# Raw cosine and sine tables turned once, the bias added in head 0, the causal mask on VectorE, fewer scatter drains, and powers three tiles behind

## The reference

```python
q  = rope(rmsnorm(x @ Wq + bq, qn_w), pos)            # per head
entries = sum over 4 tokens of softmax(x @ Wcmp + bcmp) * x      # 512 entries
ck = rope(rmsnorm(entries @ Wk + bk, kn_w), block_ends);  cv = entries @ Wv + bv
sc = q @ ck.T * scale, NEG where block_ends > pos;  top 8 of each row, softmax over them, times cv
lk = rope(rmsnorm(x @ Wlk + blk, kn_w), pos);  lv = x @ Wlv + blv
local = softmax(q @ lk.T over the own and the previous block of 128, banded) @ lv
x  = layernorm(x + ((sparse + local) / 2) @ Wo + bo)
```

```python
y = sum over the 4 picked experts of weight * (silu(x @ w1[e]) * (x @ w3[e])) @ w2[e]
x = layernorm(x + y + (silu(x @ sw1) * (x @ sw3)) @ sw2)
```

## Time and profile before

| what | us |
|---|---|
| median of three executions (2488.65 to 2490.56) | 2489.43 |
| the profiled execution, its own time | 2492.0 |
| its span, first to last instruction | 2490.2 |
| TensorE busy, share of the span | 2239.0 (90%) |
| VectorE busy | 1372.6 (55%) |
| ScalarE busy | 1172.2 (47%) |
| GpSimd busy | 1348.1 (54%) |

### The profile page before, as it was taken

The page is one execution under the profiler, slowest core; times in us unless marked ns, Lnnn a source line. Parts: engine busy times, 40 slices in busy tenths (PEclk is TensorE's granted clock), DMA queues, the critical chain, the costliest instruction groups (busy, mean ns, idle before and its releaser), DMA issues. The chain is left out here.

```text
span 2490.2 us, 45317 instructions
## 1 busy us (share of the span) xinstructions
PE 2239.0 (90%) x13489; PEld 2017.7 (81%) x13490; DVE 1372.6 (55%) x4446; ACT 1172.2 (47%) x3726; POOL 1348.1 (54%) x1942
## 2 busy tenths in 40 slices
PE   5299999999999999999999996989799999878662
PEld 3289999899899999898999995867699998768542
DVE  4266676676666667666666776382223323343257
ACT  2166666566566666666666665421133333333211
POOL 2576676666666666666666664436501103483374
PEclk8599999999999999999999999689899999989876
DMA  3140060000000000000000001214523324564164
GB/s 119 62 171 3 28 266 13 11 20 18 5 20 18 5 21 20 16 8 21 19 4 20 2 1 41 75 42 167 188 80 112 112 80 144 174 203 151 66 192 146
DMA packets 68916, 178.29 MB, mean 72 GB/s; under 512 B 11648, under 2 KB 15296, under 8 KB 68672
## 3 DMA queue, kind: packets, MB, share of 16 engines
q1 hardware_dynamic: 36864, 85.58, 10.4%
q0 software_dynamic: 19568, 69.10, 8.5%
q10 hardware_dynamic: 12240, 20.73, 2.3%
HBM read 108.26 MB, written 67.13 MB: 70 GB/s over the span
## 5 line engine op out<-in xcount | busy, mean ns | idle before, releaser
L773 POOL TENSOR_TENSOR cross<-nat,rope_tables 128x128 f32<-128x128 f32 x256 | 147.9, 578 | 446.0 <-DVE nat L635 446.0
L921 PE MATMUL bank<-whi,xT_lo 128*128 128x384 f32 x1024 | 368.7, 360 | 4.2 <-ACT v L727 3.3
L922 PE MATMUL bank<-wlo,xT_hi 128*128 128x384 f32 x1024 | 347.2, 339 | 0.0
L923 PE MATMUL bank<-whi,xT_hi 128*128 128x384 f32 x1024 | 346.4, 338 | 0.0
L1475 POOL TENSOR_TENSOR ring_lo<-staged,ring_hi 128x1088 fp32r<-128x1088 f32 x48 | 121.2, 2538 | 402.4 <-ACT ring_hi L1437 398.3
L597 DVE TENSOR_TENSOR acc<-acc,bank 128x512 f32<-128x512 f32 x256 | 176.0, 688 | 226.7 <-PE bank L923 210.0
L707 ACT COPY probT<-bank 128x128 f32<-128x128 f32 (+3 forms) x256 | 109.1, 426 | 380.2 <-PE bank L549 380.2
L921 PE MATMUL bank<-ring_hi,xslo 128*128 128x352 f32 x600 | 205.1, 342 | 29.1 <-issue 27.7
L635 DVE TENSOR_TENSOR nat<-bank,bqk 128x256 f32<-128x256 f32 x256 | 108.9, 426 | 165.0 <-PE bank L923 163.9
L921 PEld LDWEIGHTS bank<-whi,xT_lo 128*128 128x128 f32 x1024 | 193.0, 188 | 4.8 <-DVE nat L635 3.6
L923 PE MATMUL bank<-ring_hi,xshi 128*128 128x352 f32 x600 | 196.5, 328 | 0.0
(11 more groups left out here) (295 smaller groups left out, 6349.2 us busy)
## 6 DMA issues: line engine op xcount, KB each, us to landing
staged<-in_wexp POOLq DMA_DIRECT2D x60, 544.0 KB, 5.2
slots_in<-zeros SPq DMA_DIRECT2D x41, 512.0 KB, 6.0
xslot<-slots_in SPq DMA_DIRECT2D x76, 256.0 KB, 2.7
slots_out<-yslot ACTq DMA_DIRECT2D x76, 256.0 KB, 2.0
wraw<-in_wh SPq DMA_DIRECT2D x16, 768.0 KB, 4.3
staged<-in_wexp SPq DMA_DIRECT2D x20, 544.0 KB, 3.8
slots_out<-zeros SPq DMA_DIRECT2D x9, 512.0 KB, 6.1
acc<-in_x SPq DMA_DIRECT2D x4, 1024.0 KB, 14.1
```

Source lines behind the costliest of these rows:

```text
L773: pool.tensor_tensor(cross[:, :, :], nat[:, a.two, :, 0:2 * ROT], sin, ALU.mult).then_inc(s_mult, 1)
L921: pe.matmul(out, wl_, xh_, start=first, stop=False)
L922: pe.matmul(out, wh_, xl_, start=False, stop=False)
L923: return pe.matmul(out, wh_, xh_, start=False, stop=last)
```

## The change

Opening: the raw tables are loaded in one piece, cosines in rows 0 to 63 and sines in rows 64 to 127 of `cos_sin`, and turned once, one transpose a tile, between the second and the third block of entries. The norm weights are turned too (two transposes, one ScalarE copy, `nw`), and VectorE multiplies the turned tables out of the bank into `rope`, two products a chunk. GpSimd fills the 64 columns that are not turned with the norm weight and makes `cos_end` and `sin_end` from the raw tables; the second half of the sines for these comes when the first is used, by a wait on SP. ScalarE's high parts of the first head's weights stand ahead of the entry copies, GpSimd's low parts ahead of the power. VectorE's rope of the compressed keys stands ahead of the mean of squares, and the last chunk's low parts behind it. `bo` is added by GpSimd, one tile a step, in head 0, and VectorE's output sums of head 0 wait for it.

Heads: the mask matmul is gone; VectorE adds `diag`, now float32, to the last 32 score columns in the bank, and its memset waits for that. The reversed view of the sines is gone.

Front: GpSimd waits after every sixteenth transfer instead of every eighth. Combine: power(n) stands behind gather(n+3). The diff, cut; what is left out are names in signatures, semaphores and tile declarations.

```diff
@@ -98,27 +98,27 @@
-    diag = sb("diag", [P, EPT], BF16)
-    identb = sb("identb", [P, P], BF16)
+    diag = sb("diag", [P, EPT])
+    bo = sb("bo", [P, HID])
...
@@ -183,13 +180,18 @@
             for c in range(NCH):
                 sp.dma_start(acc[:, c * TPC:(c + 1) * TPC, :],
                              t["x"][c * CH:(c + 1) * CH, :].rearrange("(n p) d -> p n d", p=P)).then_inc(x_in[c], 16)
+            sp.dma_start(cos_sin[0:2 * ROT, :], t["cos"][0:2 * ROT, :]).then_inc(tab_in, 16)
+            sp.dma_start(cos_sin[2 * ROT:4 * ROT, :], t["sin"][2 * ROT:4 * ROT, :]).then_inc(tab_in, 16)
             sp.dma_start(wk[:, :, :], t["Wk"].rearrange("(k p) d -> p k d", p=P)).then_inc(k_in, 16)
+            sp.dma_start(sin[:, :], t["sin"][0:2 * ROT, 0:S // 2]).then_inc(sin_in, 16)
             sp.dma_start(wraw[:, :, :, :].rearrange("p a k d -> p (a k d)"), t["wh"][0, :, 0:3 * KC * D]).then_inc(w_in, 16)
-            sp.dma_start(bo[:, :], t["bo"].broadcast_to([P, HID])).then_inc(r_in, 16)
+            sp.dma_start(bo[:, :], t["bo"].broadcast_to([P, HID])).then_inc(bo_in, 16)
                              t["wh"][h, 0:1, 3 * KC * D + 2:HEAD_COLS].rearrange("o d -> d o")).then_inc(blv_in[h], 16)
+            sp.wait_ge(ends_done, 2)
+            sp.dma_start(sin[:, :], t["sin"][0:2 * ROT, S // 2:S]).then_inc(sin_in, 16)
             sp.wait_ge(bias_copy, 1)
...
             x_highs(0)
             act.wait_ge(bias_turn, 1)
             act.copy(bias_by_head[:, :], bank[0][0:2 * NH, 0:P]).then_inc(bias_copy, 1)
+            act.wait_ge(nw_turn, 1)
+            act.copy(nw[:, :, :], bank[1][:, 0:2 * P].rearrange("p (g d) -> p g d", g=2)).then_inc(nw_copy, 1)
+            act.copy(cos_end[2 * ROT:P, :], norm_w[2 * ROT:P, 0:1].to_broadcast([P - 2 * ROT, C])).then_inc(nw_copy, 1)
             act.wait_ge(wstep, 4)
             act.activation(by_tile[:, :], by_tile[:, :], ACT.Exp).then_inc(wexp, 1)
             for b in range(CB):
                 act.wait_ge(ent, b + 1)
                 act.copy(rows[:, b, :], bank[b][:, :]).then_inc(ent_rows, 1)
             x_highs(1)
+            act.wait_ge(w_in, 16)
+            for k in range(KC):
+                act.copy(weight_piece(whi[0], k), wraw[:, :, k, :]).then_inc(w_high, 1)
             for k in range(0, KC, 2):
                 act.wait_ge(ent_turned, k + 1)
                 act.copy(entT[:, k, :], bank[k][:, :]).then_inc(ent_act, 1)
...
         @block.tensor
-                    wait_for(pe, x_low, (c - 1) * KC + k + 1)
+                    if c == 1:
+                        pe.wait_ge(tab_sin, k + 1)
+                    else:
+                        wait_for(pe, x_low, (c - 1) * KC + k + 1)
...
-            def tables(c):
-                pe.wait_ge(tab, c + 1)
-                for i in range(TPC):
-                    if c:
-                        pe.wait_ge(tab_copy, (c - 1) * TPC + i + 1)
-                    else:
-                        pe.wait_ge(x_low, (NCH - 1) * KC + i + 1)
-                    cols = slice(i * P, (i + 1) * P)
-                    for j, src in enumerate((cosq, cosk, sin)):
-                        mm = pe.transpose(bank[4 + i][:, j * P:(j + 1) * P], src[:, cols], ident[:, :])
+            def tables():
+                pe.wait_ge(tab_in, 32)
+                for c in range(NCH):
+                    pe.wait_ge(x_low, c + 1)
+                    for i in range(TPC):
+                        n = c * TPC + i
+                        mm = pe.transpose(bank[4 + c][:, i * P:(i + 1) * P], cos_sin[:, n * P:(n + 1) * P], ident[:, :])
                     mm.then_inc(tab_turn, 1)
...
                          ident[:, :]).then_inc(bias_turn, 1)
+            pe.wait_ge(c_in, 16 * 6)
+            pe.transpose(bank[1][:, 0:P], norm_w[:, 1:2].to_broadcast([P, P]), ident[:, :])
+            pe.transpose(bank[1][:, P:2 * P], norm_w[:, 0:1].to_broadcast([P, P]), ident[:, :]).then_inc(nw_turn, 1)
...
             pe.wait_ge(bias_copy, 1)
+            pe.wait_ge(nw_copy, 1)
             for b in range(CB):
+                if b == 2:
+                    tables()
                 pe.wait_ge(wspread, b + 1)
...
         @block.gpsimd
-            def tables(c):
-                cols = slice(c * CH, (c + 1) * CH)
-                if c:
-                    pool.wait_ge(tab_turn, c * TPC)
-                pool.dma_start(cosq[:, :], t["cos"][:, cols]).then_inc(cos_in, 16)
-                pool.dma_start(sin[:, :], t["sin"][:, cols]).then_inc(sin_in, 16)
-                pool.wait_ge(cos_in, (c + 1) * 16)
-                pool.wait_ge(sin_in, (c + 1) * 16)
-                if not c:
-                    pool.wait_ge(c_in, 16 * 6)
-                pool.tensor_scalar(cosk[:, :], cosq[:, :], norm_w[:, 0:1], None, ALU.mult).then_inc(step, 1)
-                pool.tensor_scalar(sin[:, :], sin[:, :], norm_w[:, 2:3], None, ALU.mult).then_inc(step, 1)
-                pool.wait_ge(step, c * 3 + 2)
-                ends = slice(RATIO - 1, CH, RATIO)
-                out = slice(c * CH // RATIO, (c + 1) * CH // RATIO)
-                pool.tensor_copy(cos_end[:, out], cosk[:, ends]).then_inc(ends_done, 1)
-                pool.tensor_copy(sin_end[:, out], sin[0:2 * ROT, ends]).then_inc(ends_done, 1)
-                pool.tensor_scalar(cosq[:, :], cosq[:, :], norm_w[:, 1:2], None, ALU.mult).then_inc(step, 1)
-                pool.wait_ge(step, c * 3 + 3)
-                pool.nop().then_inc(tab, 1)
-
-            tables(0)
-            pool.wait_ge(ent, CB)
-            pool.wait_ge(r_in, 16)
-            pool.wait_ge(xturn, NCH * KC)
-            pool.tensor_tensor(acc[:, 0:POOL_TILES, :], acc[:, 0:POOL_TILES, :],
-                               bo[:, :].unsqueeze(1).to_broadcast([P, POOL_TILES, HID]), ALU.add)
-            pool.wait_ge(kms, 1)
-            pool.wait_ge(consts, 1)
-            pool.tensor_tensor(rstd[:, :], ms[:, :], half[:, 0:CB], ALU.pow).then_inc(krstd, 1)
+            pool.wait_ge(c_in, 16 * 6)
+            pool.wait_ge(nw_copy, 1)
+            rest = rope[:, :, 0:2 * P].rearrange("p n (g d) -> p n g d", g=2)
+            for g in range(2):
+                pool.tensor_copy(rest[:, :, g, 2 * ROT:P], nw[:, g, 2 * ROT:P].unsqueeze(1).to_broadcast([P, NT, P - 2 * ROT]))
+            ends = slice(RATIO - 1, S, RATIO)
+            pool.wait_ge(tab_in, 32)
+            pool.tensor_scalar(cos_end[0:2 * ROT, :], cos_sin[0:2 * ROT, ends], norm_w[0:2 * ROT, 0:1], None,
+                               ALU.mult).then_inc(ends_done, 1)
+            for half_ in range(2):
+                pool.wait_ge(sin_in, 16 * (half_ + 1))
+                pool.tensor_scalar(sin_end[:, half_ * (C // 2):(half_ + 1) * (C // 2)], sin[:, RATIO - 1:S // 2:RATIO],
+                                   norm_w[0:2 * ROT, 2:3], None, ALU.mult).then_inc(ends_done, 1)
             for k in range(KC):
                 pool.wait_ge(w_high, k + 1)
                 pool.tensor_tensor(weight_piece(wlo[0], k), wraw[:, :, k, :], weight_piece(whi[0], k).bitcast(F32),
                                    ALU.subtract).then_inc(w_low, 1)
-            for c in range(1, NCH):
-                tables(c)
+            pool.wait_ge(kms, 1)
+            pool.wait_ge(consts, 1)
+            pool.tensor_tensor(rstd[:, :], ms[:, :], half[:, 0:CB], ALU.pow).then_inc(krstd, 1)
...
             x_lows(0)
+            for c in range(NCH):
+                dve.wait_ge(tab_turn, c + 1)
+                if not c:
+                    dve.wait_ge(nw_copy, 1)
+                turned_tile = bank[4 + c][:, :].rearrange("p (n s d) -> p n s d", n=TPC, s=2)
+                part = rope[:, c * TPC:(c + 1) * TPC, :]
+                weights = nw[:, :, 0:2 * ROT].unsqueeze(1).to_broadcast([P, TPC, 2, 2 * ROT])
+                dve.tensor_tensor(part[:, :, 0:2 * P].rearrange("p n (g d) -> p n g d", g=2)[:, :, :, 0:2 * ROT],
+                                  turned_tile[:, :, 0:1, :].to_broadcast([P, TPC, 2, 2 * ROT]), weights, ALU.mult)
+                dve.tensor_tensor(part[:, :, 2 * P:3 * P].rearrange("p n (g d) -> p n g d", g=2),
+                                  turned_tile[:, :, 1:2, :].to_broadcast([P, TPC, 2, 2 * ROT]), weights,
+                                  ALU.mult).then_inc(tab_sin, 1)
             x_lows(1)
             for k in range(1, KC, 2):
...
             dve.wait_ge(kproj, 1)
             dve.wait_ge(ksq, 1)
-            x_lows(3)
-            dve.wait_ge(kssq, 1)
-            dve.tensor_scalar(ms[:, :], b_kssq[:, 0:CB], 1.0 / D, EPS, ALU.mult, ALU.add).then_inc(kms, 1)
-
-            dve.wait_ge(r_in, 16)
-            dve.tensor_tensor(acc[:, POOL_TILES:NT, :], acc[:, POOL_TILES:NT, :],
-                              bo[:, :].unsqueeze(1).to_broadcast([P, NT - POOL_TILES, HID]), ALU.add)
-            dve.wait_ge(vproj, 1)
-            dve.tensor_tensor(cv[:, :, :], b_vproj[:, :].rearrange("p (b d) -> p b d", b=CB),
-                              bv[:, :].unsqueeze(1).to_broadcast([P, CB, D]), ALU.add)
-
```

(41 more changed lines are left out.)

## The result

The kernel after takes 2430.32 us (median of 4, 2425.55 to 2432.81) where the kernel before takes 2489.88 beside it: ratio 0.9759, 95% interval 0.9742 to 0.9776. The forecast was 2416, its range 2400 to 2440: the sign and the range hold, 14 us are missing. The profiled execution has a span of 2427.8 us against 2490.2.

What follows compares the result with a forecast made beforehand. TensorE's issue and waits bound the heads, GpSimd's table chunks the opening, GpSimd the scatter's end, a late first power the last block. Terms -48.0 -1.2 -11.2 -13.2 = -73.6 from 2489.4 give 2416; range 2400 to 2440.

Steps and rivals of the forecast that it cites:

- Opening: Block before the heads: table transposes, copies and GpSimd's chunk loop go, ending near 67.0 instead of 115.0; -48.0 us.
- the price of the power: GpSimd's power in the opening: priced at 1 us, not its row's 6.29, because VectorE's addition beside it is gone.
- Heads: Head loops: mask matmuls -7.7, VectorE's mask link +1.5, bo additions +5; sum -1.2 us, bounds -18 and +20.
- The price of 5 us for bo: Head 0: GpSimd's bo additions can hold VectorE's L622 and L629, 0.3 us a step, 5 us.
- the rival: Head 0: each bo addition holds VectorE for its whole 1.2 us, 19 us instead of 5, giving 2430; chance 0.08.
- The mask: Head steps: 256 mask matmuls go, 0.03 us each, -7.7 us; VectorE's added operation and wait cost 1.5 us.
- The link on VectorE: Head steps: VectorE's mask addition delays what follows by 0.24 us, mostly hidden by slack; about 0.1 us a head, 1.5 us.
- Scatter: Scatter of 64 indirect transfers: four of seven drain pauses go, the last (4.68) among them; -11.2 us.
- The reading that GpSimd's tail is its own: End of scatter: 5.3 us behind GpSimd's last issue belong to GpSimd, so the next block starts about 1773.5; -11.2 us.
- Powers: Last block: power(0) follows gather(3), VectorE is let go near 2388.0, last variance near 2470.8 instead of 2484.0; -13.2 us.
- The case "slower": Head steps: the mask link exceeds its slack everywhere, needing a link of 0.7 us; slower than before, chance 0.03.
- The three terms named for the bound of -50: Range's weak end: mask costing 22 us in the heads, scatter's tail 5, opening 4 short.

Runs made afterwards that it cites:

- the last experiment: The after kernel with 128 extra TensorE waits, plus bo for tiles 6 to 11 added by VectorE beside the opening's power: 2412.96 us.
- mask on TensorE: The after kernel with the mask made by TensorE's second product again, VectorE's addition gone and two small VectorE copies in the opening: 2425.77 us.
- padded: The after kernel with 128 more waits (64 instructions) of TensorE at its very start, nothing else changed: 2409.88 us.

## Why the prediction was right, and where it was off

**Opening** (-48.0, measured -51.3). It lies just outside its bounds of -43 to -50, and the heads' first matmul, at 63.77, outside the 65 to 71 named as a sign. The mechanism and the price of the power are shown by the last experiment. The term that was off is the start of the key projection, put at 52.0 and measured at 49.92; from there the mean squares came as worked out, at 59.73 instead of 61.9. The rest is the end: the heads were put 1.2 us behind VectorE's last operation and start 0.3 behind it. The transfers, said to grow by 0.75 MB, fell over the whole program from 178.29 to 177.79 MB.

**Heads** (-1.2, measured +12.0). This is where most of the 14 us are. Over the same stretch (first matmul to last replacement) the kernels line up as before 1415.2, mask on TensorE 1419.3, padded 1407.8, after 1427.2.
- *bo and the rest,* +4.1: head 0 +3.2, the two long single heads with the lower clock +4.8, everything else -3.9 (1.7 of it ahead of the first replacement). The price of 5 us for bo stood, 4.7 to 5.3 measured, and so did its mechanism in most steps; in the two where nearly a whole addition was lost the rival was right.
- *The mask,* -11.5, or -9.9 without what the clock does; predicted -6.2. The sum is nearer than its halves only because both were mis-sized in opposite directions. For the matmul I had two readings, 0.03 by the distance of starts and 0.08 with the weight load behind it, and took the first; the runs show the size of the second (19.2 to 20.5 us, predicted 7.7). The link on VectorE costs 9.0 to 9.3 us where I had 1.5: it was not swallowed by slack, in head 0 least of all.
- *The loop's start,* +19.4: 22.0 in the ten heads of the loop, less 2.5 elsewhere, 1.6 of which is the clock in the last head. Without it the heads would stand at -7.4 and the kernel at the padded one's 2409.9, 6 us below the forecast. No step and no rival of the prediction has it. I counted what TensorE issues and what it waits for, and passed over that the change moves the whole instruction stream: the rows of "issue" at the loop starts were in the profile of before, 1.6 us each, and I took them for a constant. The written rival that gives 2430, bo holding VectorE, is not what happened; it gives the right time for a wrong reason. That the time of after lies within the range at all is in this respect luck.

**Scatter** (-11.2, measured -10.4). Undone, it costs 11.5 by the medians and 7.7 to 8.5 in its own block. The long last pause of 4.68 us, one of the term's parts, did not come back: the longest with seven pauses is 2.8. The reading that GpSimd's tail is its own holds: the 7.58 us behind its last issue are unchanged and the block moved with it. Sixteen outstanding transfers are issued as fast as eight, 0.30 us apart.

**Powers** (-13.2, measured -14.1). Undone, they cost 13.0 (12.1 in the block), and the wait of 18.9 us comes back.

The case "slower" would have needed 0.7 us of link in every step; nothing came near it. Of the range, -90 to -50, the time lies at -59.6 by the medians and -62.4 by the profiles: room left for other causes, above all 20 us for the mask, took up the loop's start. The three terms named for the bound of -50 (mask 22, tail 5, opening 4 short) come to about -44 if they all fall together, so the written bound was too narrow for its own reasons.

## What to carry to other kernels

An edit that adds or removes instructions ahead of a loop moves the loop's start in the instruction stream, and with it what each jump back costs. Compare the "issue" waits at the loop starts before and after every such edit, and if a new one appears between two pieces of one instruction, shift the start by some tens of slots, tell the jump, or write the loop out. A matmul that is small by its own columns can cost more behind it than at its own place (0.075 us here, 0.03 of it by the distance of starts), so price it by a step with and without it. Before two profiles are compared head by head, look at the granted clock of each head: one stretch at the lower level is worth as much as the term that is being measured. Where an operation moves to an engine with slack, the slack has to be read where it is least, at the first and last tiles and wherever another engine holds it.

## What was not expected of the hardware

- 128 waits for data long there, 64 instructions of nothing, take 20 us off a kernel of 2430. An instruction of padding costs about 0.11 us where nothing hides it: in after TensorE's first matmul comes at 16.85 with 64 of them and at 34.42 with 224 (in before at 25.55 with 129).
- The first pause behind a jump back is 1.4 to 1.9 us on TensorE at most starts (2.1 to 3.3 at one or two starts in seven of the runs). The other engines pause beside it: VectorE 2.9 to 3.8 us, ScalarE mostly 1.9 to 2.9, GpSimd mostly 1.6 to 1.9. The second, if a boundary follows within some six instructions by the account above, is 2.4 to 2.9, and the clock is low for 3.4 or 6.8 us beside or behind it. With some 38 instructions ahead of the boundary 0.4 to 1.1 us are left of it, at four of five starts.
- Telling the jump (2396.25) does as well as writing the loop out (2398.95).
- In the routed experts TensorE has 26.4 us of "issue" in after's profile page. Nearly all are four pauses of 6.4 us, over twice as long as those at the heads' loop and there in before too. What they are is not known, and telling those jumps was not tried:

```profile
L926 PE MATMUL bank<-ring_hi,xslo 128*128 128x352 f32 x600 | 205.6, 343 | 27.8 <-issue 26.4
...
2080.70 0.65 PE L926 MATMUL bank<-ring_hi,xslo 128*128 128x352 f32 x1 [6.39 <-issue]
```
